# A new order of stages for every engine of a two-layer transformer kernel, and GpSimd's squares and products in halves

## The chip, the core and the metric

One core of a Trainium2 chip runs the whole program in one launch. The metric is device microseconds (us), the median of three runs. Engines are named TensorE (PE; its weight loads PEld), VectorE (DVE), ScalarE (ACT), GpSimd (POOL) and SyncE (SP, which only issues DMAs here). Each takes its instructions strictly in the order in which the program lists them, and waits on semaphores for the others.

## The reference

The input is 32 entries of 256 tokens by 128 channels, float32. Per entry, with layer norm in front of each layer:

```python
xn = _layernorm(x, axis=-1)
x = x + _L0_attn_ref(xn, ...) + _L0_ffn_ref(xn, ...)
xn = _layernorm(x, axis=-1)
x = x + _L1_attn_ref(xn, ...) + _L1_ffn_ref(xn, ...)
```

`_L0_attn_ref` is 16-head attention over normalised q and k whose weight is `(1 - arccos(clip(q.k)) / pi) ** 16`, divided by the row sum. `_L0_ffn_ref` is a second 16-head attention, with softmax, plus a mixture of 8 experts of which the gate picks 2. `_L1_attn_ref` is causal single-head attention. `_L1_ffn_ref` is a gated MLP (128 to 352 to 128) whose operands are rounded to FP4 in blocks of 16 along the last axis. No entry needs another.

## The kernel before

Weights are prepared once (transposes, FP4 rounding), up to about 50 us. Then the program runs steps t = -1 to 33. The work on an entry is cut into stages, and the table `ORDER` holds for each engine a list of `(stage, argument, lag)`: in step t the engine does that stage for entry t + lag. A stage with lag +1 is so done a step ahead of one with lag 0, and lag -2 is the last. `steps` unrolls steps -1, 0, 1 and the last ones and loops over two steps at a time between them; items whose entry doesn't exist are skipped. The lists are the only thing that sets the order; nothing is moved at run time.

The stages that matter here, in the order in which an entry goes through them:

- `load` (SP), `ln0` (VectorE moments, ScalarE a first guess of 1/sd), `rstd0` (VectorE refines it, L774 to L776), `xnT` (VectorE writes the normalised tile `xn`, L781; TensorE transposes it; ScalarE copies it to `xnT`), `proj` 0 and 1 (TensorE; ScalarE copies one bank, VectorE the other, L802).
- `gmax`, `gexp`, `choose` 0 to 4: the gate. `choose` 1 is a copy of 4 numbers a row, L836.
- `norm`, `guess`, `newton`, `unit`, `high`, `stack`, `stackT`: q and k are normalised, cut into a float16 high and low part (ScalarE or GpSimd copy the high part, GpSimd subtracts, L566) and transposed.
- `m` 0 to 7: scores whose row maximum VectorE takes (L885); `maxT`: these maxima are cut into bfloat16 parts by VectorE (L897 to L900), transposed by TensorE and copied by ScalarE; `e` 0 to 7: the scores again less the maximum, ScalarE's exponential (`prob`); `pvf`: their product with v.
- `c` 0 to 7: cosines, which VectorE clips into `curve` (L879). For each of four pairs: `sq` (GpSimd squares, L530), `ln` and `sigm` (ScalarE), `mul` (curve times root: pairs 0 and 2 on GpSimd, L533; 1 and 3 on VectorE, L875), `arctan`, `wln`, `wexp` (ScalarE), `pvw`. `table` 0 and 1 load ScalarE's function table before the logarithms and the sigmoids.
- `experts` 0 and 1 (TensorE; VectorE adds 16 tiles, L859), `finf`, `finc`, `ocT`, `wo`: outputs of layer 0.
- `ln1` (as `ln0`; ScalarE writes `rstd1`), `rstd1`, `xn1T`, `quantx` 0 to 8 (FP4 rounding in nine small steps; step 7 is L452), `xqT`, `p1`, `gu`, `hmul`, `quanth` 0 to 8, `hT`, `s1`, `s1e`, `p1T`, `o1`, `down`, and the store from SP.

Scores go through two PSUM slots in turn (`SCORES`), and all else of TensorE through two banks in turn (`MISC`), both counted in the order of TensorE's list: a stage on TensorE waits (`bank_read`) until what used its slot or bank last has been read. A new list for TensorE therefore changes these waits too.

GpSimd's two stages that the change touches are the `sq` and `mul` branches of its `run`.

## Time and profile before

| | before |
|---|---|
| median of 3 runs | 1975.3 us (1971.95 to 1977.01) |
| the profiled execution | 1968.91 us, its span 1967.1 us |
| busy over the span | ACT 1778.4, DVE 1761.1, PE 1475.6, POOL 1183.2 us |
| mean granted TensorE clock | 0.856 |
| time from step to step, t = 1 to 32 | 57.61 us (1786.0 us over 31 steps) |

The span is nearly all repetition: a step of every engine, 31 times over, with a ramp of some 70 us in front (weights, steps -1 and 0) and the drain of the last entry behind. So the time is read from one step. A time stamp in the rows is in us from the span's start; "idle before" is time in which the engine stood, with what ended it behind the arrow. Two rows of one engine can overlap by about 0.1 us, since an instruction starts while the one ahead of it is ending.

### The profile page before, as it was taken

What the parts mean: (1) busy time and instruction counts of PE and PEld (TensorE: products, weight loads), DVE (VectorE), ACT (ScalarE), POOL (GpSimd) and SP (SyncE); (2) the same over time, 40 slices, a digit from 0 to 9 for tenths busy, and PEclk for the clock granted to TensorE, in tenths of its full rate; (3) what the DMA queues carried; (4) which work ended last, traced back from release to release, by engine and by line L of the source; (5) the groups of instructions that cost most, each with busy time, mean ns of one, the idle gap of its engine ahead of it and who ended that gap; (6) DMA issues with size and microseconds to landing.
All of it is one profiled execution on the core that took longest, in us unless ns stands there. A gap on an engine that the chain in (4) does not pass through costs nothing.

```text
span 1967.1 us, 38505 instructions
## 1 busy us (share of the span) xinstructions
PE 1475.6 (75%) x12022; PEld 751.1 (38%) x12022; DVE 1761.1 (90%) x3977; ACT 1778.4 (90%) x1888; POOL 1183.2 (60%) x540
## 2 busy tenths in 40 slices
PE   2677778777778777777878777778778778777765
PEld 1223434333443433344343334434334434333333
DVE  5779998999999999999999999999999999999864
ACT  1299999999999999999999999999999999999993
POOL 1556666666666666666666656665666666665640
PEclk9667898889888988988898888898888888888876
DMA  1000000000000000000000000000000000000000
GB/s 42 3 4 1 6 1 6 5 6 6 6 5 0 6 5 6 6 6 5 0 6 5 6 6 6 0 6 6 5 6 5 6 0 6 6 5 6 4 3 6
DMA packets 21058, 11.19 MB, mean 6 GB/s; under 512 B 1431, under 2 KB 20953, under 8 KB 20956
## 3 DMA queue, kind: packets, MB, share of 16 engines
q1 hardware_dynamic: 20956, 10.20, 1.8%
q14 instruction: 83, 0.68, 0.1%
...
## 4 chain that ended last, share of the span: by engine, by line
DVE 37%; issue 22%; ACT 20%; PE 18%; DVEq 2%; SPq 0%; POOL 0%; ACTq 0%; DMA 0%; POOLq 0%
ACT curve L578 10%; DVE nmax L885 6%; DVE curve L875 5%; ACT root L578 4%; PE psM L1045 4%; DVE curve L879 3%; PE psM L1037 3%; DVE acc L859 3%; DVE xn L781 1%; PE psS L1095 1%; DVE h L454 1%; PE psM L1207 1%; PE psM L1190 1%; DVE stkT L871 1%; ACT prob L578 1%
## 5 line engine op out<-in xcount | busy, mean ns | idle before, releaser
L530 POOL TENSOR_TENSOR root<-curve 128x2048 f32<-128x2048 f32 x128 | 478.9, 3741 | 453.2 <-DVE curve L879 453.2
L578 ACT ACTIVATE curve<-curve 128x2048 f32<-128x2048 f32 x384 | 719.1, 1907 | 5.6 <-POOL curve L533 2.2
L578 ACT ACTIVATE root<-root 128x2048 f32<-128x2048 f32 x256 | 484.7, 1906 | 0.0
L533 POOL TENSOR_TENSOR curve<-curve,root 128x2048 f32<-128x2048 f32 x64 | 354.6, 5562 | 65.2 <-ACT root L578 65.2
L879 DVE TENSOR_SCALAR curve<-psS 128x1024 f32<-128x1024 f32 x256 | 308.2, 1215 | 2.7 <-PE psS L1068 1.9
L885 DVE TENSOR_REDUCE nmax<-psS 128x4 f32<-128x1024 f32 x256 | 302.7, 1213 | 0.9 <-PE psS L1077 0.9
L578 ACT ACTIVATE prob<-psS 128x1024 f32<-128x1024 f32 x256 | 256.6, 1029 | 32.8 <-PE psS L1097 31.1
L566 POOL TENSOR_TENSOR stk<-qk,stk 128x512 f16<-128x512 f32 x128 | 148.1, 1167 | 73.4 <-ACT stk L578 72.9
L1045 PE MATMUL psM<-we,xnT 128*128 128x512 f32 x256 | 172.4, 762 | 0.0
L875 DVE TENSOR_TENSOR curve<-curve,root 128x2048 f32<-128x2048 f32 x64 | 161.0, 2516 | 6.1 <-ACT root L578 6.1
L1077 PE MATMUL psS<-stkT 32*128 32x256 f16 x1024 | 103.1, 294 | 80.7 <-DVE curve L879 42.5
L1221 PE MATMUL psV<-curve,vc 128*32 128x256 f32 x2048 | 134.1, 391 | 26.1 <-ACT curve L578 22.4
L1190 PE MATMUL psM<-wguT,xqT 128*128 128x352 f32 x256 | 124.6, 624 | 36.3 <-ACT hqT L578 32.9
L1221 PE MATMUL psV<-prob,vf 128*32 128x256 f32 x2048 | 151.0, 417 | 0.6 <-ACT prob L578 0.6
L859 DVE SCALAR_TENSOR_TENSOR acc<-psM,comb,acc 128x128 f32<-128x128 f32 x512 | 136.8, 337 | 12.2 <-PE psM L1045 11.8
L1207 PE MATMUL psM<-wdT,hqT 128*128 128x128 f32 (+1 forms) x384 | 88.6, 416 | 64.1 <-DVE h L977 63.4
L1068 PE MATMUL psS<-stkT 32*128 32x256 f16 x1024 | 105.6, 316 | 22.6 <-DVE curve L879 11.7
L1207 PEld LDWEIGHTS psM<-wdT,hqT 128*128 128x128 f32 (+1 forms) x384 | 79.4, 312 | 77.9 <-DVE h L977 76.8
L1056 PE MATMUL psM<-ident,stk 128*128 128x128 f16 x1024 | 81.8, 225 | 33.6 <-ACT xn1T L578 25.8
L1095 PE MATMUL psS<-stkT 32*128 32x256 f16 x1024 | 102.8, 300 | 3.4 <-ACT prob L578 2.3
L1097 PE MATMUL psS<-mT,pickb 32*128 32x256 bf16 x1024 | 102.2, 299 | 0.0
L1221 PEld LDWEIGHTS psV<-curve,vc 128*32 128x32 f32 x2048 | 59.9, 110 | 98.0 <-issue 71.7
...
## 6 DMA issues: line engine op xcount, KB each, us to landing
...
```

The costliest lines, as they stand in the source:

```text
L530: nc.gpsimd.tensor_tensor(root[:, two], curve[:, p, two], curve[:, p, two], ALU.mult).then_inc(s_sq, 1)
L533: nc.gpsimd.tensor_tensor(curve[:, p, two], curve[:, p, two], root[:, two], ALU.mult).then_inc(s_half[0], 1)
L566: nc.gpsimd.tensor_tensor(lo, src, hi, ALU.subtract).then_inc(s_stk, 1)
L578: return nc.scalar.activation(out, in_, func, **kw)
L859: nc.vector.scalar_tensor_tensor(acc[:, p, j, :], bank[:, (e % 4) * D:(e % 4 + 1) * D], comb[:, p, j, e:e + 1], acc[:, p, j, :], ALU.mult, ...
L875: nc.vector.tensor_tensor(curve[:, p, two], curve[:, p, two], root[:, two], ALU.mult).then_inc(s_half[1], 1)
L879: nc.vector.tensor_scalar(curve[:, p, arg * UC:(arg + 1) * UC], psS[:, slot_of(stage, arg), :, :, :].rearrange("p a k q -> p (a k q)"), CO ...
L885: nc.vector.tensor_reduce(nmax[:, :, 2 * arg:2 * arg + 2].rearrange("p j a -> p a j"), psS[:, slot_of(stage, arg), :, :, :], AX.X, ALU.max ...
L1045: mm(bank[:, :], xnT[:, j * P:(j + 1) * P], we[:, 4 * arg:4 * arg + 4, :].rearrange("p e f -> p (e f)"), start=False, stop=True).then_inc( ...
L1190: ins = mm(bank[:, 0:I], xqT[:, arg * P:(arg + 1) * P], wguT[:, m, :], start=True, stop=True)
L1207: ins = mm(bank[:, j * D:(j + 1) * D], hqT[0:CH[c], j, c, :], wdT[0:CH[c], c, :], start=(c == 0), stop=(c == NCH - 1))
L1221: ins = mm(psV[rows(hh), kind, half, :], head_window(v, p, kt, head_at(g, hh)), w[:, hh, kt, :], start=(g % 2 == 0 and kt == 0), stop=(g % ...
```

## The change

Every engine but SP gets a new list. Each list is turned (a step now begins with `wln` 1 on ScalarE, `experts` 0 on VectorE, `c` 4 on TensorE, and `sq` 1 on GpSimd), so a few stages have another lag, and the stages inside are permuted. GpSimd's `sq` and `mul` over 2048 elements a row become two instructions over 1024 each; the semaphore is raised by the second.

```diff
@@ -56,44 +56,43 @@
         ("load", 0, 1), ("down", 0, -2),
     ],
     "tensor": [
-        ("c", 2, 0), ("s1", 0, -2), ("finf", 0, -1), ("c", 3, 0), ("c", 4, 0), ("experts", 0, 0), ("c", 5, 0),
-        ("pvw", 0, -1), ("c", 6, 0), ("experts", 1, 0), ("pvw", 1, -1), ("pvw", 2, -1), ("p1T", 0, -2),
-        ("pvw", 3, -1), ("xnT", 0, 1), ("maxT", 0, 0), ("c", 7, 0), ("proj", 0, 1), ("e", 0, 0), ("proj", 1, 1),
-        ("e", 1, 0), ("finc", 0, -1), ("o1", 0, -2), ("ocT", 0, -1), ("e", 2, 0), ("e", 3, 0), ("wo", 0, -1),
-        ("pvf", 0, 0), ("e", 4, 0), ("e", 5, 0), ("pvf", 1, 0), ("xn1T", 0, -1), ("e", 6, 0), ("e", 7, 0),
-        ("stackT", 0, 1), ("stackT", 1, 1), ("pvf", 2, 0), ("m", 0, 1), ("m", 1, 1), ("p1", 0, -1), ("m", 2, 1),
-        ("stackT", 2, 1), ("pvf", 3, 0), ("stackT", 3, 1), ("m", 3, 1), ("xqT", 0, -1), ("m", 4, 1), ("hT", 0, -2),
-        ("hT", 1, -2), ("c", 0, 1), ("gu", 0, -1), ("m", 5, 1), ("m", 6, 1), ("gu", 1, -1), ("c", 1, 1), ("m", 7, 1),
-        ("down", 0, -2),
+        ("c", 4, 0), ("s1", 0, -2), ("experts", 0, 0), ("pvw", 0, -1), ("c", 5, 0), ("c", 6, 0), ("maxT", 0, 0),
+        ("experts", 1, 0), ("e", 0, 0), ("e", 1, 0), ("pvw", 1, -1), ("pvw", 2, -1), ("p1T", 0, -2), ("c", 7, 0),
+        ("xnT", 0, 1), ("pvw", 3, -1), ("proj", 0, 1), ("proj", 1, 1), ("e", 2, 0), ("o1", 0, -2), ("e", 3, 0),
+        ("finc", 0, -1), ("pvf", 0, 0), ("hT", 0, -2), ("e", 4, 0), ("ocT", 0, -1), ("e", 5, 0), ("wo", 0, -1),
+        ("hT", 1, -2), ("pvf", 1, 0), ("e", 6, 0), ("stackT", 0, 1), ("e", 7, 0), ("stackT", 1, 1), ("m", 0, 1),
+        ("xn1T", 0, -1), ("m", 1, 1), ("m", 2, 1), ("stackT", 2, 1), ("pvf", 2, 0), ("m", 3, 1), ("stackT", 3, 1),
+        ("m", 4, 1), ("pvf", 3, 0), ("m", 5, 1), ("xqT", 0, -1), ("p1", 0, -1), ("c", 0, 1), ("gu", 0, -1),
+        ("c", 1, 1), ("m", 6, 1), ("gu", 1, -1), ("c", 2, 1), ("m", 7, 1), ("finf", 0, 0), ("down", 0, -2),
+        ("c", 3, 1),
     ],
     "vector": [
-        ("c", 2, 0), ("s1", 0, -2), ("finf", 0, -1), ("quanth", 1, -2), ("c", 3, 0), ("c", 4, 0), ("quanth", 2, -2),
-        ("experts", 0, 0), ("c", 5, 0), ("quanth", 3, -2), ("ln0", 0, 1), ("c", 6, 0), ("experts", 1, 0),
-        ("quanth", 4, -2), ("rstd0", 0, 1), ("quanth", 5, -2), ("xnT", 0, 1), ("maxT", 0, 0), ("quanth", 6, -2),
-        ("quanth", 7, -2), ("c", 7, 0), ("proj", 0, 1), ("proj", 1, 1), ("gmax", 0, 1), ("quanth", 8, -2),
-        ("finc", 0, -1), ("o1", 0, -2), ("norm", 0, 1), ("wo", 0, -1), ("ln1", 0, -1), ("rstd1", 0, -1),
-        ("choose", 0, 1), ("xn1T", 0, -1), ("quantx", 0, -1), ("newton", 0, 1), ("quantx", 1, -1), ("quantx", 2, -1),
-        ("choose", 1, 1), ("quantx", 3, -1), ("quantx", 4, -1), ("stackT", 0, 1), ("quantx", 5, -1),
-        ("quantx", 6, -1), ("stackT", 1, 1), ("choose", 2, 1), ("quantx", 7, -1), ("m", 0, 1), ("m", 1, 1),
-        ("quantx", 8, -1), ("p1", 0, -1), ("choose", 3, 1), ("m", 2, 1), ("stackT", 2, 1), ("stackT", 3, 1),
-        ("m", 3, 1), ("m", 4, 1), ("mul", 1, 0), ("c", 0, 1), ("hmul", 0, -1), ("m", 5, 1), ("m", 6, 1),
-        ("mul", 3, 0), ("hmul", 1, -1), ("choose", 4, 1), ("quanth", 0, -1), ("c", 1, 1),
-        ("m", 7, 1), ("down", 0, -2),
+        ("experts", 0, 0), ("c", 5, 0), ("c", 6, 0), ("ln0", 0, 1), ("experts", 1, 0), ("rstd0", 0, 1),
+        ("quanth", 5, -2), ("xnT", 0, 1), ("quanth", 6, -2), ("c", 7, 0), ("quanth", 7, -2), ("proj", 0, 1),
+        ("quanth", 8, -2), ("proj", 1, 1), ("gmax", 0, 1), ("o1", 0, -2), ("finc", 0, -1), ("choose", 0, 1),
+        ("norm", 0, 1), ("wo", 0, -1), ("ln1", 0, -1), ("rstd1", 0, -1), ("xn1T", 0, -1), ("newton", 0, 1),
+        ("stackT", 0, 1), ("quantx", 0, -1), ("stackT", 1, 1), ("quantx", 1, -1), ("choose", 1, 1), ("quantx", 2, -1),
+        ("quantx", 3, -1), ("m", 0, 1), ("quantx", 4, -1), ("choose", 2, 1), ("quantx", 5, -1), ("quantx", 6, -1),
+        ("quantx", 7, -1), ("m", 1, 1), ("choose", 3, 1), ("quantx", 8, -1), ("choose", 4, 1), ("m", 2, 1),
+        ("stackT", 2, 1), ("m", 3, 1), ("stackT", 3, 1), ("m", 4, 1), ("m", 5, 1), ("p1", 0, -1), ("mul", 1, 0),
+        ("c", 0, 1), ("hmul", 0, -1), ("c", 1, 1), ("m", 6, 1), ("mul", 3, 0), ("m", 7, 1), ("hmul", 1, -1),
+        ("c", 2, 1), ("quanth", 0, -1), ("finf", 0, 0), ("quanth", 1, -1), ("maxT", 0, 1), ("quanth", 2, -1),
+        ("down", 0, -2), ("quanth", 3, -1), ("c", 3, 1), ("quanth", 4, -1), ("s1", 0, -1), ("c", 4, 1),
     ],
     "scalar": [
-        ("table", 0, -1), ("wln", 0, -1), ("wln", 1, -1), ("wexp", 0, -1), ("s1e", 0, -2), ("wexp", 1, -1),
-        ("wln", 2, -1), ("wexp", 2, -1), ("wln", 3, -1), ("ln0", 0, 1), ("wexp", 3, -1), ("p1T", 0, -2), ("ln", 0, 0),
-        ("xnT", 0, 1), ("maxT", 0, 0), ("ln", 1, 0), ("proj", 0, 1), ("oC", 0, -1), ("e", 0, 0), ("proj", 1, 1),
-        ("e", 1, 0), ("ln", 2, 0), ("ocT", 0, -1), ("gexp", 0, 1), ("e", 2, 0), ("e", 3, 0), ("guess", 0, 1),
-        ("ln1", 0, -1), ("e", 4, 0), ("e", 5, 0), ("ln", 3, 0), ("xn1T", 0, -1), ("e", 6, 0), ("high", 2, 1),
-        ("e", 7, 0), ("high", 3, 1), ("table", 1, 0), ("p1", 0, -1), ("sigm", 0, 0), ("sigm", 1, 0), ("xqT", 0, -1),
-        ("sigm", 2, 0), ("hT", 0, -2), ("hT", 1, -2), ("arctan", 0, 0), ("gu", 0, -1), ("sigm", 3, 0), ("oF", 0, 0),
-        ("arctan", 1, 0), ("gu", 1, -1), ("arctan", 2, 0), ("arctan", 3, 0),
+        ("wln", 1, -1), ("wexp", 0, -1), ("wln", 2, -1), ("wexp", 1, -1), ("wexp", 2, -1), ("maxT", 0, 0),
+        ("wln", 3, -1), ("s1e", 0, -2), ("ln0", 0, 1), ("e", 0, 0), ("wexp", 3, -1), ("p1T", 0, -2), ("xnT", 0, 1),
+        ("e", 1, 0), ("oC", 0, -1), ("proj", 0, 1), ("ln", 0, 0), ("proj", 1, 1), ("e", 2, 0), ("ln", 1, 0),
+        ("gexp", 0, 1), ("e", 3, 0), ("hT", 0, -2), ("ocT", 0, -1), ("e", 4, 0), ("e", 5, 0), ("guess", 0, 1),
+        ("hT", 1, -2), ("ln1", 0, -1), ("e", 6, 0), ("e", 7, 0), ("ln", 2, 0), ("high", 2, 1), ("ln", 3, 0),
+        ("high", 3, 1), ("xn1T", 0, -1), ("table", 1, 0), ("sigm", 0, 0), ("sigm", 1, 0), ("xqT", 0, -1),
+        ("p1", 0, -1), ("sigm", 2, 0), ("sigm", 3, 0), ("gu", 0, -1), ("oF", 0, 0), ("arctan", 0, 0),
+        ("arctan", 1, 0), ("arctan", 2, 0), ("gu", 1, -1), ("arctan", 3, 0), ("table", 0, 0), ("wln", 0, 0),
     ],
     "gpsimd": [
-        ("fadd", 0, -1), ("sq", 2, 0), ("sq", 3, 0), ("norm", 0, 1), ("high", 0, 1), ("high", 1, 1), ("stack", 0, 1),
-        ("stack", 1, 1), ("unit", 0, 1), ("stack", 2, 1), ("stack", 3, 1), ("residual", 0, 1), ("mul", 0, 0),
-        ("mul", 2, 0), ("sq", 0, 1), ("sq", 1, 1),
+        ("sq", 1, 0), ("fadd", 0, -1), ("sq", 2, 0), ("sq", 3, 0), ("norm", 0, 1), ("high", 0, 1), ("high", 1, 1),
+        ("stack", 0, 1), ("stack", 1, 1), ("unit", 0, 1), ("stack", 2, 1), ("stack", 3, 1), ("mul", 0, 0),
+        ("mul", 2, 0), ("residual", 0, 1), ("sq", 0, 1),
     ],
 }
 MOST_LAG = max(-lag for order in ORDER.values() for s, a, lag in order)
@@ -523,14 +522,16 @@
             pool.wait_ge(s_wcp, SETUP_USES)
 
             def run(stage, arg, b, p, t):
-                two = slice(arg * 2 * UC, (arg + 1) * 2 * UC)
+                one, other = (slice((2 * arg + k) * UC, (2 * arg + k + 1) * UC) for k in range(2))
                 if stage == "sq":
                     pool.wait_ge(s_clip, due(s_clip, b, 2 * arg + 2))
                     pool.wait_ge(*half_done(b - 1, arg))
-                    nc.gpsimd.tensor_tensor(root[:, two], curve[:, p, two], curve[:, p, two], ALU.mult).then_inc(s_sq, 1)
+                    nc.gpsimd.tensor_tensor(root[:, one], curve[:, p, one], curve[:, p, one], ALU.mult)
+                    nc.gpsimd.tensor_tensor(root[:, other], curve[:, p, other], curve[:, p, other], ALU.mult).then_inc(s_sq, 1)
                 if stage == "mul" and arg not in HALF_ON_DVE:
                     pool.wait_ge(s_sig, due(s_sig, b, arg + 1))
-                    nc.gpsimd.tensor_tensor(curve[:, p, two], curve[:, p, two], root[:, two], ALU.mult).then_inc(s_half[0], 1)
+                    nc.gpsimd.tensor_tensor(curve[:, p, one], curve[:, p, one], root[:, one], ALU.mult)
+                    nc.gpsimd.tensor_tensor(curve[:, p, other], curve[:, p, other], root[:, other], ALU.mult).then_inc(s_half[0], 1)
                 if stage == "residual":
 
                     pool.wait_ge(s_x[p], due(s_x[p], b, LANDED[p]))
```

## Rows read from the trace of the kernel before

**Rows 1.** The page: busy us of each engine (share of the span) xinstructions.

```profile
PE 1475.6 (75%) x12022; PEld 751.1 (38%) x12022; DVE 1761.1 (90%) x3977; ACT 1778.4 (90%) x1888; POOL 1183.2 (60%) x540
```

**Rows 2.** One line's instructions (min/median/max ns): the table load that opens a step.

```profile
L609 ACT ACT_TABLE_LOAD  x32: 1283/1283/1283, 124.4 to 1910.4; - x32
```

**Rows 3.** Stretches (us, busy and count by engine, clock): 23 steps; half clock.

```profile
411.90:1739.70 1327.80, 1035.65 (x8627) 529.25 (x8627) 1241.20 (x2807) 1268.43 (x1335) 846.97 (x368) 0.87 0.02 5
...
1228.00:1231.40 3.40, 3.40 (x5) 0.77 (x4) 3.36 (x8) 3.37 (x3) 2.96 (x2) 0.50 0.01 2
```

**Rows 4.** Waits in 411.9 to 1739.7: us in total, times, longest.

```profile
ACT prob L578 <- PE psS L1097: 22.3, 43, 1.3
ACT ocT L578 <- PE psM L1122: 16.7, 23, 1.0
```

**Rows 5.** Timeline of ScalarE in one step (start, length, [idle before]).

```profile
1236.48 0.38 ACT L578 ACTIVATE xnT<-psM 128x256 f32<-128x256 f32 x1
1237.33 0.38 ACT L578 ACTIVATE mT<-psM 128x256 bf16<-128x256 bf16 x1 [0.47 <-PE psM L1087]
...
1249.39 0.20 ACT L578 ACTIVATE lnv<-mv 128x2 f32<-128x2 f32 x1 [0.16 <-DVE mv L768]
1249.62 0.20 ACT L578 ACTIVATE rstd<-lnv 128x2 f32<-128x2 f32 x1
1249.81 1.94 ACT L578 ACTIVATE prob<-psS 128x1024 f32<-128x1024 f32 x2
1251.63 1.91 ACT L578 ACTIVATE root<-root 128x2048 f32<-128x2048 f32 x1
...
1254.60 0.65 ACT L578 ACTIVATE stk<-qk 128x512 f16<-128x512 f32 x1
...
1294.53 0.37 ACT L578 ACTIVATE xnT<-psM 128x256 f32<-128x256 f32 x1
```

**Rows 6.** Timeline of VectorE in the same step.

```profile
1235.70 0.23 DVE L897 CAST mstk<-nmax 128x32 bf16<-128x32 f32 x1
...
1236.49 0.30 DVE L900 TENSOR_TENSOR mstk<-nres,mstk 128x32 bf16<-128x32 f32 x1
...
1249.86 0.16 DVE L774 SCALAR_TENSOR_TENSOR lnt<-mv,rstd 128x2 f32<-128x2 f32 x1 [0.51 <-ACT rstd L578]
...
1250.33 0.16 DVE L831 TENSOR_REDUCE gs<-ge 128x2 f32<-128x16 f32 x1
...
1256.29 0.47 DVE L452 SCALAR_TENSOR_TENSOR xq<-xqT,xq 128x256 f32<-128x256 f32 x1
...
1290.02 1.90 DVE L859 SCALAR_TENSOR_TENSOR acc<-psM,comb,acc 128x128 f32<-128x128 f32 x7 [0.36 <-PE psM L1045]
...
1293.16 0.59 DVE L781 TENSOR_SCALAR xn<-xt,mv,rstd 128x128 f32<-128x128 f32 x2
```

**Rows 7.** One line's instructions each: VectorE beside GpSimd (min/median/max ns).

```profile
L836 DVE COPY best<-top x32: 160/892/896, 55.9 to 1833.8; 128x4 f32<-128x4 f32 x32
L452 DVE SCALAR_TENSOR_TENSOR xq<-xqT,xq x32: 424/592/1296, 161.5 to 1940.5; 128x256 f32<-128x256 f32 x32
L875 DVE TENSOR_TENSOR curve<-curve,root x64: 2279/2466/4924, 113.2 to 1904.2; 128x2048 f32<-128x2048 f32 x64
```

**Rows 8.** One line's instructions each: GpSimd's prices (min/median/max ns).

```profile
L530 POOL TENSOR_TENSOR root<-curve x128: 3601/3602/4181, 70.2 to 1877.7; 128x2048 f32<-128x2048 f32 x128
L533 POOL TENSOR_TENSOR curve<-curve,root x64: 4519/5556/6616, 109.2 to 1899.4; 128x2048 f32<-128x2048 f32 x64
L543 POOL TENSOR_TENSOR qsq<-qk x32: 1041/1773/1776, 50.2 to 1823.3; 128x512 f32<-128x512 f32 x32
```

**Rows 9.** Timeline of TensorE: one expert matmul pair at each clock.

```profile
1222.04 1.13 PE L1045 MATMUL psM<-we,xnT 128*128 128x512 f32 x2
...
1227.79 1.95 PE L1045 MATMUL psM<-we,xnT 128*128 128x512 f32 x2
```

**Rows 10.** Timeline of ScalarE in the ramp, step 0.

```profile
81.75 0.20 ACT L578 ACTIVATE lnv<-mv 128x2 f32<-128x2 f32 x1 [23.34 <-DVE mv L768]
```

## The prediction

> **What bounds the kernel now.** First the page: ScalarE and VectorE are each busy for 90% of the span, TensorE for 75%, GpSimd for 60% [rows 1]. So no transfer matters, and the question is what lies in the idle tenth of the two. Next the period: the table load that opens ScalarE's step comes 32 times, from 124.4 to 1910.4 us [rows 2], so a step takes 1786.0 / 31 = 57.61 us. In the 23 steps from 411.9 to 1739.7, ScalarE is busy 1268.43 / 23 = 55.15 us a step and VectorE 1241.20 / 23 = 53.97 us [rows 3]. A new order can't take less than ScalarE's 55.15 us, so at most 2.5 us a step are to be had. ScalarE's largest waits are for TensorE's scores, 22.3 / 23 = 0.97 us a step, and for the transposed output, 0.73 us [rows 4].
>
> Then the timelines, for the loop that sets the period; the reader is to see that two engines hand it to each other. ScalarE writes the second layer norm's rstd at 1249.82 [rows 5]; VectorE, which stood 0.51 us for it, goes on at 1249.86 and works through most of its list until the next entry's `xn` is written at 1293.75 [rows 6]. That is stretch A, 43.93 us. TensorE transposes it and ScalarE takes it at 1294.53, 0.78 us later [rows 5]. From `xnT` at 1236.48 to rstd at 1249.82 ScalarE then has stretch C, 13.34 us, in which VectorE has slack. 43.93 + 0.78 + 13.34 = 58.05, within 0.8% of the mean step. A microsecond that VectorE waits in A, or ScalarE in C, is a microsecond of the period; the other way round it is hidden.
>
> **The change, part by part.**
>
> **Stretch A.** Comparing the two lists of VectorE from `rstd1` to `xnT`: the new one has all stages of the old, plus `maxT`, less `choose` 0. `maxT` costs 1.09 us from first to last, about 1.0 with the overlap [rows 6]; `choose` 0 is three short overlapping instructions, the first 0.16 us long [rows 6], some 0.2 in all. In the old list `choose` 1, a copy of 4 numbers, takes 0.89 us where 0.16 would do [rows 7], since GpSimd works on the same memory beside it; in the new list it falls into a gap of GpSimd (after `unit`, before the third `stack`): -0.73. The two multiplications of VectorE took 2.47 where 2.28 is their least [rows 7], 2 x 0.19 = 0.37; I find them at the end of a GpSimd product in the new order too, but with halves the rest to wait for is shorter: 0.2 stays, so -0.2. The wait for experts of 0.36 [rows 6] goes, if TensorE is at 2.4 GHz there. Sum: 43.93 + 1.0 - 0.2 - 0.73 - 0.2 - 0.36 = 43.4 us. I take 43.5, with 0.1 for `xn1T` standing right behind `rstd1`. Bounds: 43.2 if no wait is left, 44.7 if as much time is lost to GpSimd as now (0.73 + 0.37) and 0.2 more.
>
> **Stretch C.** Of the 13.34 us five waits, of which the first, 0.47, and the last, 0.16, stand in the rows, make 2.37 [rows 5]; 10.97 are work. The new list has in C five exponentials for four (+0.91, half of the 1.82 us from start of two to the next instruction), `hT` twice (+0.76), and not `maxT` (-0.28): 12.36; with two waits less, 0.2 more is saved by overlap. Three waits remain in the new list: for `proj` 0, which TensorE now has behind `pvw` 3; for `e` 2, behind `proj` 1; and for `ocT`, behind `e` 4. Before, `e` and `ocT` alone made 0.97 + 0.73 [rows 4]; I put all three at half of that, 0.85, an estimate. 12.16 + 0.85 = 13.0 us. Bounds: 12.5 with 0.3 of waits, 14.5 with the 2.37 of now.
>
> **What ScalarE itself needs in A.** What C gains in work ScalarE's part of A loses (1.4 us), so its path has 1.4 us of cover there. That hides a new wait: TensorE now has `xqT` behind `m` 5, which waits for VectorE to read `m` 3; `p1`, `c` 0 and `gu` are queued behind it, and ScalarE stands up to 0.7 us for `xqT`. If VectorE is over 1 us late there, the cover is used up.
>
> The table load with `wln` 0, and `finf`, only change the step in which they are counted. SP's list is as it was: its loads wait for sums two entries back, its stores for `down`, and neither is near the loop.
>
> **GpSimd in halves.** Of a square of 512 elements (1.041 us at the least) and one of 2048 (3.602) [rows 8] I work out 1.67 ns an element and 0.19 us that each instruction costs by itself. Six more instructions a step cost 1.1 us, between 0 (if they overlap) and 2. GpSimd is busy 846.97 / 23 = 36.8 us of 57.6 [rows 3], so this is hidden unless `arctan` 2 waits for it. The first product starts with ScalarE's `sigm` 0, some 10.0 us after rstd; two products of 4.52 + 0.15 [rows 8] with one of VectorE's between them (2.28) end at 21.6. ScalarE's own list reaches `arctan` 2 at 20.4 without waits and 21.1 with `xqT`'s: 0.5 to 1.2 us, inside its cover of 1.4. If that cover is gone, it is paid.
>
> **Ramp and drain.** In step 0 ScalarE stands 23.34 us before `ln0` [rows 10]. With `maxT` a step earlier it can do two exponentials in that time, 1.8 us, and VectorE's `xn` comes earlier: 3 us, between 0 and 6. The drain is one entry's chain in both: 0.
>
> **The clock.** Between 1228.0 and 1231.4 the granted clock is 0.50, so 1.2 GHz [rows 3], and a pair of expert matmuls takes 1.95 us against 1.13 [rows 9]. The new list puts TensorE's work from `finf` through `stackT` 1 close together, and I take 2.4 GHz for it.
> The Trainium skill ("TensorE: Matmul & The Clock Gate", Part 1: The HAM clock gate) says that for modelling the ramp penalty is under 1% of a typical kernel's span and shouldn't be fitted. By that rule an order laid with the clock in it brings under 20 us, and the result stays near the time before. The trace agrees for the time and not for the share: the mean clock is 0.87, yet ScalarE's two waits above come to 1.7 us a step.
>
> **The sum.** 43.5 + 0.78 + 13.0 = 57.3 us a step, 0.3 less than 57.61; over 31 steps -10, with the ramp -13. The profiled execution took 1968.9 us (span 1967.1 and 1.8 around it), so 1956 us; the median of the runs is 6.4 us above that execution, so the median should be 1962 us. With the gain between -1.1 and +0.9 us a step, 1935 to 2002.
>
> **The rivals.**
>
> *GpSimd's last subtraction gets in front of `quantx` 7 (slower).* In the old step L452 comes 6.43 us after L774 [rows 6]. In the new list `m` 0 stands ahead of it (+1.13), `choose` 0 doesn't (-0.22), nor `choose` 1's wait (-0.73), with 0.1 for the gap: 6.7 us after rstd. GpSimd's last `stack` starts when ScalarE's last `high` is done: two exponentials (1.82), two logarithms of 1.91 less the overlap of 0.1, and two copies of 0.65, the first less its overlap [rows 5]: 6.6 us, and the start. If GpSimd is first, VectorE waits for all of that instruction, as in the executions of L452 that took up to 1296 ns instead of 424 [rows 7]. 0.85 us a step: +0.55 net, 31 x 0.55 - 3 = +14, so 1989 us. It decides at less than 0.1 us, and half of L452's executions took under 592 ns: 25%.
> The Trainium skill ("SBUF — State Buffer", SBUF: two separate sides) calls the pair of ports that VectorE and GpSimd share an exclusive lock: whoever starts first has it for the whole instruction. By that rule the loser pays all of the rest, in each step alike, which is this rival; the trace agrees, with 0.89 us for the copy of 4 numbers.
>
> *TensorE falls to 1.2 GHz in the dense part (slower).* Both halves of `experts` 1 wait for reads by VectorE and ScalarE; at 1.95 for 1.13 us a pair [rows 9] the second bank is two times 0.82, 1.6 us, late, and VectorE waits in A. +1.3 us a step net, 31 x 1.3 - 3 = +37: 2012 us. It decides when TensorE has stood for VectorE's `hmul` 1 and the clock has not come back by `experts` 1. 9%.
>
> *ScalarE takes over (no change).* The waits for `xqT`, the products and TensorE use up its 1.4 us of cover: 57.6 us a step, 1972 to 1975 us. For it: ScalarE reached 1294.53 without any wait, so it was as late as VectorE. 16%.
>
> *The order holds better than I find (faster).* No wait of VectorE on GpSimd, a third of those in C: 43.2 + 0.78 + 12.5 = 56.5, -34 - 3: 1938 us. 10%.
>
> **How the numbers follow.** My forecast, 1962 us, has 40% (its own range 1948 to 1974). A measurement can't tell 0.3%, 6 us, from no change. Faster by more: most of the forecast's 40% and the last rival, 48%. Within: the third rival and the edges of its neighbours, 20%. Slower: the first two and the far part of the third, 32%. The range 1935 to 2002 leaves out the worst of the clock and more than 56.5.
>
> **What would show it.** ScalarE's table loads 57.3 us apart; L836 at 0.16 us; L452 near 424 ns (near 1296 ns: the first rival); ScalarE's waits for scores and `ocT` together under 1.0 us a step; L1045 near 1.13 us a pair throughout (1.95: the second rival). GpSimd busy about 1.1 us a step longer. I am wrong at the root if stretch A isn't what ends the step, which waits of VectorE inside A would show.

## The result, and the profile after

The changed kernel takes 1992.8 us (median of 4 runs, 1991.9 to 1996.2) against 1973.7 us of the kernel before on the same chip: a ratio of 1.0095, with a 95% interval of 1.0077 to 1.0112. It is slower by 1%, where 1962 us was predicted. The profiled execution took 1993.0 us, with a span of 1991.2.

The page's busy line answers to [rows 1]:

```profile
PE 1513.1 (76%) x12022; PEld 748.9 (38%) x12022; DVE 1763.2 (89%) x3977; ACT 1774.6 (89%) x1888; POOL 1253.6 (63%) x732
```

VectorE and ScalarE do what they did before, in 24 us more of span. The table load that opens ScalarE's step (now L610) answers to [rows 2]:

```profile
L610 ACT ACT_TABLE_LOAD  x32: 1283/1283/1283, 129.2 to 1933.7; - x32
```

So a step takes (1933.7 - 129.2) / 31 = 58.21 us where it took 57.61: 18.5 of the 24 us. The first load comes 4.8 us later, and after the last one 57.5 us follow for 56.7. The loss is in the loop, and some of it in the ramp.

One line's instructions each (min/median/max ns), against [rows 7] and [rows 8]; line numbers in the helper for fp4 have gone down by one, most of the others up by one:

```profile
L837 DVE COPY best<-top x32: 159/165/167, 57.2 to 1855.5; 128x4 f32<-128x4 f32 x32
...
L451 DVE SCALAR_TENSOR_TENSOR xq<-xqT,xq x32: 424/1341/1416, 167.7 to 1963.2; 128x256 f32<-128x256 f32 x32
...
L876 DVE TENSOR_TENSOR curve<-curve,root x64: 2280/2346/3603, 117.0 to 1923.9; 128x2048 f32<-128x2048 f32 x64
...
L529 POOL TENSOR_TENSOR root<-curve x128: 1884/1894/3937, 69.1 to 1897.3; 128x1024 f32<-128x1024 f32 x128
```

The copy of 4 numbers is at its least (0.89 us before), but `quantx` 7 (L451) now takes 1.34 us in the median, where 0.42 would do. ScalarE's waits from 420 to 1770 us (in total, times, longest), to be read beside [rows 4]:

```profile
ACT xqT L579 <- PE psM L1183: 48.6, 23, 2.7
ACT prob L579 <- PE psS L1098: 5.5, 16, 0.5
ACT u1T L579 <- PE psM L1146: 4.1, 14, 0.5
ACT ocT L579 <- PE psM L1123: 4.0, 23, 0.2
```

The waits for scores and for `ocT` are nearly gone (1.70 us a step before, 0.41 now), and one for `xqT` of 2.1 us a step has come, where the old kernel's was under 0.1. What happens on VectorE and GpSimd around `quantx` 7 (timeline of one step; ScalarE's rstd ended at 1326.75):

```profile
1332.94 0.42 DVE L449 SCALAR_TENSOR_TENSOR xq<-xqT,xq 128x256 f32<-128x256 f32 x1
1333.40 1.40 DVE L451 SCALAR_TENSOR_TENSOR xq<-xqT,xq 128x256 f32<-128x256 f32 x1
1334.73 1.21 DVE L886 TENSOR_REDUCE nmax<-psS 128x4 f32<-128x1024 f32 x1
```

```profile
1333.36 1.16 POOL L567 TENSOR_TENSOR stk<-qk,stk 128x512 f16<-128x512 f32 x1 [1.16 <-ACT stk L579]
```

GpSimd's last `stack` starts 0.04 us ahead of `quantx` 7, which then ends 0.28 us after it. In all 23 steps from 411.9 to 1739.7 us it starts ahead, by 0.04 to 0.10 us. ScalarE a little later in the same step:

```profile
1336.69 1.90 ACT L579 ACTIVATE root<-root 128x2048 f32<-128x2048 f32 x1
1340.16 0.38 ACT L579 ACTIVATE xqT<-psM 128x256 f32<-128x256 f32 x1 [1.58 <-PE psM L1183]
1340.69 0.38 ACT L579 ACTIVATE u1T<-psM 128x256 f32<-128x256 f32 x1 [0.15 <-PE psM L1146]
```

TensorE has `xqT` behind `m` 5, which waits until VectorE has read `m` 3. VectorE comes to `m` 3 later by what `quantx` 7 lost.

The prediction measured one step of the old kernel in three pieces. The same three over the 23 middle steps of either kernel, from the starts of ScalarE's `xnT`, the ends of its second rstd and the ends of VectorE's `xn`:

| us a step | step measured then | before, mean of 23 | forecast | after, mean of 23 |
|---|---|---|---|---|
| stretch A (rstd to `xn`) | 43.93 | 44.15 | 43.5 | 44.70 |
| TensorE's transposes and `xnT` | 0.78 | 1.00 | 0.78 | 0.87 |
| stretch C (`xnT` to rstd) | 13.34 | 12.58 | 13.0 | 12.58 |
| sum | 58.05 | 57.73 | 57.3 | 58.15 |

The three pieces lie end to end, so they add up to the step by definition; what counts is which of them changed. A has grown, C is what it was. The steps aren't alike: 11 of the 23 take 57.4 to 57.6 us, the others up to 59.7.

### The profile page after: what moved, and what is told of

The parts are those of the page before. It is cut to its first block and busy times, and to the rows that moved or that the text cites. A ratio compares the mean times of both kernels' runs of the same rounds, so it can differ in the third digit from the quotient of the medians.

```text
span 1991.2 us, 38613 instructions
## 1 busy us (share of the span) xinstructions
PE 1513.1 (76%) x12022; PEld 748.9 (38%) x12022; DVE 1763.2 (89%) x3977; ACT 1774.6 (89%) x1888; POOL 1253.6 (63%) x732
## 5 line engine op out<-in xcount | busy, mean ns | idle before, releaser
L579 ACT ACTIVATE curve<-curve 128x2048 f32<-128x2048 f32 x384 | 710.2, 1903 | 7.9 <-POOL curve L534 7.0
L529 POOL TENSOR_TENSOR root<-curve 128x1024 f32<-128x1024 f32 x128 | 266.3, 2081 | 305.5 <-DVE curve L880 305.5
L533 POOL TENSOR_TENSOR curve<-curve,root 128x1024 f32<-128x1024 f32 x64 | 193.4, 3022 | 147.9 <-ACT root L579 147.9
L579 ACT ACTIVATE prob<-psS 128x1024 f32<-128x1024 f32 x256 | 255.9, 1024 | 15.8 <-PE psS L1098 13.6
L1078 PE MATMUL psS<-stkT 32*128 32x256 f16 x1024 | 131.0, 347 | 181.0 <-DVE stkT L872 71.3
L530 POOL TENSOR_TENSOR root<-curve 128x1024 f32<-128x1024 f32 x128 | 261.4, 2042 | 0.0
L1222 PE MATMUL psV<-prob,vf 128*32 128x256 f32 x2048 | 178.2, 478 | 0.0
L1046 PE MATMUL psM<-we,xnT 128*128 128x512 f32 x256 | 156.0, 694 | 0.0
L534 POOL TENSOR_TENSOR curve<-curve,root 128x1024 f32<-128x1024 f32 x64 | 152.6, 2385 | 0.0
L1078 PEld LDWEIGHTS psS<-stkT 32*128 32x128 f16 x1024 | 32.3, 100 | 279.4 <-DVE nmax L886 124.7
L1096 PE MATMUL psS<-stkT 32*128 32x256 f16 x1024 | 115.0, 281 | 4.4 <-ACT prob L579 4.2
L1114 PE MATMUL psM<-ident,oFs 128*128 128x128 f32 x128 | 34.1, 422 | 110.1 <-DVE h L978 110.1
L1098 PE MATMUL psS<-mT,pickb 32*128 32x256 bf16 x1024 | 113.1, 278 | 0.0
L1057 PE MATMUL psM<-ident,stk 128*128 128x128 f16 x1024 | 101.2, 257 | 5.4 <-POOL stk L567 5.3
```

What stands on the lines that cost most here:

```text
L529: nc.gpsimd.tensor_tensor(root[:, one], curve[:, p, one], curve[:, p, one], ALU.mult)
L530: nc.gpsimd.tensor_tensor(root[:, other], curve[:, p, other], curve[:, p, other], ALU.mult).then_inc(s_sq, 1)
L533: nc.gpsimd.tensor_tensor(curve[:, p, one], curve[:, p, one], root[:, one], ALU.mult)
L534: nc.gpsimd.tensor_tensor(curve[:, p, other], curve[:, p, other], root[:, other], ALU.mult).then_inc(s_half[0], 1)
L579: return nc.scalar.activation(out, in_, func, **kw)
L1046: mm(bank[:, :], xnT[:, j * P:(j + 1) * P], we[:, 4 * arg:4 * arg + 4, :].rearrange("p e f -> p (e f)"), start=False, stop=True).then_inc( ...
```

## The experiments

Each ratio is against the kernel before, run on the same chip beside it. The changed kernel stands at 1.0095.

### The lock on `quantx` 7

```diff
-        ("quantx", 7, -1), ("m", 1, 1), ("choose", 3, 1), ("quantx", 8, -1), ("choose", 4, 1), ("m", 2, 1),
+        ("m", 1, 1), ("quantx", 7, -1), ("choose", 3, 1), ("quantx", 8, -1), ("choose", 4, 1), ("m", 2, 1),
```

> The new order, with VectorE's m 1 (a read of PSUM) one place ahead of quantx 7 (L451), so that quantx 7 comes after GpSimd's last stack. Theory (the lock on quantx 7 is the loss, and it also makes TensorE's xqT late for ScalarE): L451 falls from a mean of 1.28 us to under 0.5, ScalarE's wait for xqT from 2.1 to about 1.2 us a step, and a step takes about 0.85 us less, so 31 x 0.85 = 26 us: 1966 us, ratio to the kernel before 0.996. Rival (ScalarE's own work and another wait set the step, and VectorE only fills what is left): L451 falls just the same, but the time stays within 6 us of 1993, ratio 1.007 to 1.012.

Measured: 1975.3 us, ratio 0.9999 (0.9985 to 1.0014). `quantx` 7 and the table load:

```profile
L451 DVE SCALAR_TENSOR_TENSOR xq<-xqT,xq x32: 407/415/424, 167.8 to 1940.3; 128x256 f32<-128x256 f32 x32
...
L610 ACT ACT_TABLE_LOAD  x32: 1283/1283/1283, 128.3 to 1911.5; - x32
```

One exchange of two neighbours gives back the whole loss: the last GpSimd subtraction now runs beside a read of PSUM, which it doesn't hold up (VectorE, then GpSimd):

```profile
1203.00 1.22 DVE L886 TENSOR_REDUCE nmax<-psS 128x4 f32<-128x1024 f32 x1
```

```profile
1203.08 1.15 POOL L567 TENSOR_TENSOR stk<-qk,stk 128x512 f16<-128x512 f32 x1 [1.16 <-ACT stk L579]
```

The gain is 0.96%, 19 us, between the theory's 26 and the rival's 6, nearer to the theory. The exchange also frees the slot of `m` 1 earlier, so the ratio alone doesn't single out the lock. Steps of the short kind do: stretch A takes 44.1 to 44.3 us in them with the lock and 43.15 to 43.3 without, 1.0 us less, and nearly all of that is the length of `quantx` 7 itself (1.34 to 1.40 us for 0.41). The wait for `xqT` only fell to 1.5 us a step, and the steps come in two kinds: 11 of the 23 take 56.5 to 56.6 us, 12 take 58.0 to 58.3. What makes the others long is taken up below.

### Work for ScalarE while `xqT` is late

```diff
-        ("high", 3, 1), ("xn1T", 0, -1), ("table", 1, 0), ("sigm", 0, 0), ("sigm", 1, 0), ("xqT", 0, -1),
-        ("p1", 0, -1), ("sigm", 2, 0), ("sigm", 3, 0), ("gu", 0, -1), ("oF", 0, 0), ("arctan", 0, 0),
+        ("high", 3, 1), ("xn1T", 0, -1), ("table", 1, 0), ("sigm", 0, 0), ("sigm", 1, 0), ("sigm", 2, 0),
+        ("xqT", 0, -1), ("p1", 0, -1), ("sigm", 3, 0), ("gu", 0, -1), ("oF", 0, 0), ("arctan", 0, 0),
```

> The new order, with ScalarE's sigm 2 (1.9 us) ahead of xqT, so that ScalarE has work while TensorE's xqT is late; quantx 7 stays locked. Theory (VectorE's stretch A sets the step, ScalarE only just keeps up): the wait for xqT goes from 2.1 us a step to under 0.5, but only what ScalarE is late at xnT comes back, 0.87 less 0.63 us, some 0.25 us a step with the 1.2 GHz steps a little more: 6 to 16 us, 1977 to 1987 us, ratio 1.002 to 1.007. Rival (ScalarE's wait for xqT is itself the loss): 1.5 us a step or more, under 1950 us, ratio under 0.99.

Measured: 2036.9 us, ratio 1.0312 (1.0287 to 1.0338). Neither the theory nor the rival had it: 44 us were lost, not 6 to 16 won. The wait for `xqT` did go, to 0.45 us a step, but another took its place:

```profile
ACT curve L579 <- DVE curve L876: 55.6, 23, 2.7
...
ACT xqT L579 <- PE psM L1183: 10.4, 13, 0.9
```

The timelines of GpSimd and of VectorE's multiplication in one step show why:

```profile
1245.03 2.37 POOL L533 TENSOR_TENSOR curve<-curve,root 128x1024 f32<-128x1024 f32 x1 [2.34 <-ACT root L579]
1247.35 2.37 POOL L534 TENSOR_TENSOR curve<-curve,root 128x1024 f32<-128x1024 f32 x1
1249.66 2.37 POOL L533 TENSOR_TENSOR curve<-curve,root 128x1024 f32<-128x1024 f32 x1
1251.97 4.43 POOL L534 TENSOR_TENSOR curve<-curve,root 128x1024 f32<-128x1024 f32 x1
```

```profile
1250.58 3.59 DVE L876 TENSOR_TENSOR curve<-curve,root 128x2048 f32<-128x2048 f32 x1
```

With `sigm` 2 done early, GpSimd's second product follows the first without a gap. VectorE's multiplication arrives in its first half and takes 3.59 us for 2.28; the second half then takes 4.43 for 2.35. The multiplication ends 2.1 us after the first half, and the second half 2.2 us after the multiplication: each waited for the other in turn. In the changed kernel the wait for `xqT` had held GpSimd back: there the second product starts 0.5 to 1.4 us behind VectorE's multiplication in all 23 steps.

> Both edits: m 1 ahead of quantx 7, and sigm 2 ahead of xqT. Theory (VectorE is the limit until the lock is gone, then both are within 0.3 us): a step of 57.0 to 57.2 us, that is 26 + 8 us off 1993, 1959 us with 1952 to 1966 as bounds, ratio 0.990 to 0.996. Rival (one limit alone): no better than the better one of the two edits by itself, within 4 us.

This was both edits. Measured: 2039.8 us, ratio 1.0325 (1.0298 to 1.0353), no better than the second alone, and far from what the theory and the rival said: the multiplications are slow in this kernel too (a median of 4.2 us for the first). The test of the explanation holds the second product until VectorE's first multiplication is done:

```diff
                     pool.wait_ge(s_sig, due(s_sig, b, arg + 1))
+                    if arg == 2:
+                        pool.wait_ge(*half_done(b, 1))
```

> Both first edits (m 1 ahead of quantx 7, sigm 2 ahead of xqT), and GpSimd's second product waits until VectorE's first multiplication is done. Theory (the 43 us that sigm 2 ahead of xqT cost came only from GpSimd's second product, which then started straight behind the first and took the memory from VectorE's multiplication, 3.1 to 3.6 us instead of 2.28): both multiplications are back at 2.3 to 2.5 us, a step takes 56.5 to 57.6 us, 1944 to 1980 us, ratio 0.984 to 1.003. Rival (moving sigm 2 costs by ScalarE's own order, u1T and gu being later): over 2015 us, ratio over 1.02.

Measured: 1988.4 us, ratio 1.0061 (1.0037 to 1.0085). Of the 3.25 points the hold brings back 2.6; the first multiplication is at 2.28 us again (the second at 2.60 to 2.67). So the collision on GpSimd was the loss of the second experiment. The time is still 8 us above the theory's range: every one of the 23 steps now takes 58.0 us, the long kind, and in each the granted clock stands at 0.50 from about 17.5 to 27.7 us after `xnT`. What is left goes with the clock; that ScalarE's order has no part in it was not tested.

### The two halves of the change, alone

> The new order, but GpSimd's squares and products whole again, as before. Theory (the halves are hidden and beside the point; the loss is the order's): 1993 us within 6, ratio 1.006 to 1.013, GpSimd busy about 1.1 us a step less, VectorE's two multiplications (L876) up to 0.2 us a step longer. Rival (the halves cost the time, by more starts of GpSimd that get in front of VectorE): over 6 us faster, ratio under 1.006. Other rival (the halves are what lets VectorE's multiplications in): over 10 us slower, ratio over 1.014.

The new order with whole GpSimd instructions: 2000.2 us, ratio 1.0132 (1.0107 to 1.0157). The halves don't cost; with the new order they seem worth some 7 us, by intervals that just overlap. What they gain is in stretch C (13.25 us whole, 12.58 in halves), and some of it is lost again in A (44.45 whole, 44.70 in halves). ScalarE's waits in the kernel with whole instructions, from 420 to 1770 us, are:

```profile
ACT ocT L577 <- PE psM L1121: 9.7, 23, 0.4
ACT hqT L577 <- PE psM L1197: 6.9, 21, 0.4
```

With halves `ocT` has 4.0 and `hqT` doesn't appear.

> The old order, with GpSimd's squares and products as two instructions each (the other part of the change alone). Theory (the halves alone matter little: they add 1.1 us a step to GpSimd, hidden, and let VectorE's two multiplications in up to 0.2 us sooner): 0 to 0.4 us a step less, 1963 to 1976 us, ratio 0.994 to 1.001. Rival (each additional start of a GpSimd instruction is one more chance to get in front of VectorE): 0.3 us a step or more, ratio over 1.005.

The old order with halves: 1978.1 us, ratio 1.0015 (1.0001 to 1.0028), near no change. So the loss is the order's.

### What makes the long steps

TensorE in a long step of the kernel with `m` 1 first (`xnT` at 1410.10, the next at 1468.21):

```profile
1423.38 0.62 PE L1057 MATMUL psM<-ident,stk 128*128 128x128 f16 x8
1426.21 0.39 PE L1078 MATMUL psS<-stkT 32*128 32x256 f16 x4 [2.22 <-DVE stkT L872]
1426.54 0.44 PE L1139 MATMUL psM<-ident,xn 128*128 128x128 f32 x2
1426.90 0.39 PE L1078 MATMUL psS<-stkT 32*128 32x256 f16 x4
1428.09 0.60 PE L1078 MATMUL psS<-stkT 32*128 32x256 f16 x4 [0.79 <-DVE nmax L886]
1428.63 1.03 PE L1057 MATMUL psM<-ident,stk 128*128 128x128 f16 x8
1429.59 1.94 PE L1222 MATMUL psV<-prob,vf 128*32 128x256 f32 x16
...
1435.90 0.69 PE L1183 MATMUL psM<-ident,xq 128*128 128x128 f32 x2
```

After idle stretches of 2.22 and 0.79 us the same `m` takes 0.60 for 0.39, `stackT` 1.03 for 0.62, `pvf` 1.94 for 1.07: that is 1.2 for 2.4 GHz. From `m` 2 on TensorE is busy throughout and late with `xqT`, which comes 25.8 to 26.0 us after `xnT` in long steps and 24.4 to 24.9 in short ones. The two idle stretches alone don't make a step long: four short steps of this kernel have them as well. The stretch from 20 to 28 us after `xnT` in a short step (`xnT` at 1353.49) and in this long one; the columns are the stretch, its length, busy time and count of PE, PEld, DVE, ACT and POOL, the granted clock, and DMA:

```profile
1373.50:1381.50 8.00, 7.87 (x68) 3.58 (x60) 8.00 (x13) 7.27 (x7) 5.26 (x4) 0.84 0.00 0
1430.10:1438.10 8.00, 8.00 (x64) 3.75 (x56) 7.01 (x12) 5.34 (x6) 4.95 (x3) 0.53 0.00 1
```

In all 23 steps of that kernel: 0.78 or more in this stretch goes with 56.45 to 56.62 us, 0.57 or less with 58.0 to 58.3. The changed kernel itself has the same split: 0.79 or more with 57.4 to 57.6 us (11 steps), 0.62 or less with 57.9 to 59.7 (12 steps). In the kernel before, the same stretch, in which its `xqT` lies too, had 0.94 or more in all 23 steps: the new order brought the fall into this chain. All this is a correlation. Four kernels moved work to test it, and three then added to TensorE's activity without moving any.

```diff
-        ("m", 4, 1), ("pvf", 3, 0), ("m", 5, 1), ("xqT", 0, -1), ("p1", 0, -1), ("c", 0, 1), ("gu", 0, -1),
+        ("m", 4, 1), ("m", 5, 1), ("xqT", 0, -1), ("p1", 0, -1), ("pvf", 3, 0), ("c", 0, 1), ("gu", 0, -1),
```

> The new order with m 1 ahead of quantx 7 (as in the first experiment), and TensorE's pvf 3 (1.07 us at 2.4 GHz, 1.93 at 1.2) moved from between m 4 and m 5 to behind p1, so that it is not ahead of xqT and p1. In the first experiment the steps came in two kinds, 56.5 us and 58.1 us, the long ones with a clock of 0.65 from m 2 to xqT against 1.00. Theory (in the long steps TensorE at 1.2 GHz is late with xqT for ScalarE and with p1 for VectorE): the long steps lose 1.2 us or more, mean step 56.5 to 56.9, 1944 to 1958 us, ratio 0.984 to 0.991. Rival (the long steps come from elsewhere, and the clock only goes with them): the two kinds stay, 1968 to 1978 us, ratio 0.997 to 1.002. Other rival (ScalarE's earlier sigm 2 lets GpSimd's second product in front of VectorE's multiplication, as in the second experiment): over 1985 us, ratio over 1.005.

Measured, with `m` 1 first: 1974.0 us, ratio 0.9995 (0.9979 to 1.0010). The wait for `xqT` halved (17.7 us in 23 steps), but the mean step stayed at 57.6 us (57.4 before the move). That is the first rival's time, but the two kinds didn't stay as they were. The clock still fell in the chain, and in 12 of the 23 steps once more 51 to 52 us after `xnT`; those 12 take 57.8 to 58.0 us, and the waits for scores and experts grew. Of the steps without that second fall, one in which the first lasts from 17.2 to 27.4 us takes 57.1 us, and two in which it lasts to 30.6 take 59.2. A lighter chain alone doesn't cure the long steps.

```diff
-        ... ("e", 7, 0), ("stackT", 1, 1), ("m", 0, 1),
-        ("xn1T", 0, -1), ("m", 1, 1), ("m", 2, 1), ("stackT", 2, 1), ("pvf", 2, 0), ("m", 3, 1), ("stackT", 3, 1),
-        ("m", 4, 1), ("pvf", 3, 0), ("m", 5, 1), ("xqT", 0, -1), ...
+        ... ("e", 7, 0), ("stackT", 1, 1), ("pvf", 2, 0), ("pvf", 3, 0), ("m", 0, 1),
+        ("xn1T", 0, -1), ("m", 1, 1), ("m", 2, 1), ("stackT", 2, 1), ("m", 3, 1), ("stackT", 3, 1),
+        ("m", 4, 1), ("m", 5, 1), ("xqT", 0, -1), ...
```

> The new order with m 1 ahead of quantx 7, and TensorE's pvf 2 and pvf 3 moved out of the m chain into the gap of 2.2 us in which TensorE stands between stackT 1 and m 0. In the three kernels seen with m 1 ahead, a step is 56.5 us long where the granted clock falls to 0.50 some 17 us after xnT for 3.4 to 6.9 us, and 58.0 to 58.3 us where it stays there for 10.2 us. Theory (1.2 GHz in the m chain, with the two pvf in it, is what makes the long steps; with the gap filled and the chain light it no longer matters): every step 56.4 to 56.8 us, 1942 to 1955 us, ratio 0.983 to 0.990. Rival (the clock falls anyway, and what is late moves on to gu or to experts): steps of 57.4 us and more, ratio over 0.994.

> The new order with the two pvf moved into the gap ahead of m 0 alone, quantx 7 where the change put it. Theory (the lock and the clock are two separate losses): the lock on L451 stays at 1.3 us, the long steps of 58.4 to 59.6 go, every step is 57.4 to 57.6 us, 1968 to 1978 us, ratio 0.997 to 1.002. Rival (the long steps of the changed kernel come from the lock, by the later m chain, not from the clock): 1985 us or more, ratio over 1.005.

> All edits: m 1 ahead of quantx 7, sigm 2 ahead of xqT with GpSimd's second product held until VectorE's first multiplication is done, and the two pvf in the gap ahead of m 0. With the hold alone, every step had 10.2 us at a granted clock of 0.50 and took 58.0 us. Theory (VectorE's list sets the step once lock and clock are out of the way, ScalarE has over 1 us of cover): 56.3 to 56.7 us a step, within 4 us of the kernel with the two pvf moved but without sigm 2 and hold, ratio 0.983 to 0.990. Rival (ScalarE and VectorE are both at their limit there, and ScalarE's earlier sigm 2 brings more): 55.8 us a step or less, ratio under 0.978. Other rival (GpSimd's second product ends too late for arctan 2): over 57.2 us a step, ratio over 0.994.

With `m` 1 first: 1981.7 us, ratio 1.0041 (1.0025 to 1.0058). With the lock kept: 1990.9 us, 1.0088 (1.0061 to 1.0116). With `sigm` 2 and the hold: 1991.3 us, 1.0094 (1.0066 to 1.0122). By their times all three go to a rival: the fall moves from 17 to between 19 and 21 us after `xnT` and then mostly lasts until 29 to 31, over `xqT`, `p1` and `gu`. The reasons that the rivals gave aren't all borne out. In the second, with the lock kept, the granted clock is at 0.50 from 20 to 28 us after `xnT` in every step, so its steps of 58.0 us don't show the lock without the clock. In the third GpSimd's product, which its rival blamed, is not among ScalarE's larger waits; the largest is for `gu`, 54.4 us. In the first VectorE waits for experts, 17.5 us from 420 to 1770 us where the kernel of the first experiment has 0.3:

```profile
DVE acc L860 <- PE psM L1046: 17.5, 20, 1.1
```

In these kernels, moving work only moved the fall. The next kernel adds activity and moves nothing: TensorE repeats `stackT` 1 and `m` 1, the same result in the same place, before anyone reads it.

```diff
-                    for g in range(4):
+                    for g in 3 * list(range(4)) if arg == 1 else range(4):
...
-                    for qt_ in range(NT):
+                    for qt_ in list(range(NT)) * {1: 3}.get(arg, 1):
```

> The new order with m 1 ahead of quantx 7, every list as in the first experiment, and TensorE does some work again, with the same result in the same place: the transposes of stackT 1 three times (1.2 us more, in the gap of 2.2 us ahead of m 0) and m 1 three times (0.8 us more, in the gap ahead of m 2). VectorE reads neither before the repeats are done. So nothing changes but TensorE's activity. Theory (TensorE's idle time ahead of the m chain is what the fall of the clock follows, and the clock is what makes the long steps): the fall comes later than 17 us after xnT or is shorter, and the share of long steps (58.0 us and more, 12 to 14 of 23) falls; if all go, 56.5 us a step, 1946 us, ratio 0.986; over half gone, under 0.994. Rival (the fall only moves, as with the two pvf, and gu or experts are late instead): 57.5 us a step or more, ratio 0.998 to 1.006.

Measured, with `m` 1 first: 1958.0 us (1957.1 to 1958.9), ratio 0.9909 (0.9887 to 0.9930). TensorE in one step, and the table load:

```profile
1363.26 0.39 PE L1078 MATMUL psS<-stkT 32*128 32x256 f16 x4 [1.33 <-DVE stkT L872]
1363.59 0.44 PE L1139 MATMUL psM<-ident,xn 128*128 128x128 f32 x2
1363.95 0.83 PE L1078 MATMUL psS<-stkT 32*128 32x256 f16 x12
1365.13 0.39 PE L1078 MATMUL psS<-stkT 32*128 32x256 f16 x4 [0.35 <-DVE nmax L886]
```

```profile
L610 ACT ACT_TABLE_LOAD  x32: 1283/1283/1283, 130.5 to 1898.2; - x32
```

The idle stretches are down to 1.33 and 0.35 us. In 20 of the 23 steps the fall is later or lasts about 3 us; 4 steps are long where 12 were, and the mean step is 57.02 us by the table loads. Nothing but TensorE's own activity differs from the first experiment, and the two kinds keep their lengths (most short steps 56.5 to 56.6 us, and 58.1 to 58.3 in the three that still have the long fall in the chain). So the clock is a cause of the long steps, and having fewer of them is worth 0.9% of the time. This version is faster than both kernels.

> As the kernel with stackT 1 and m 1 three times, and m 2, m 3 and m 4 twice as well (0.39 us each at 2.4 GHz, 0.60 at 1.2). Theory (with TensorE busy throughout the m chain the clock stays, and at 2.4 GHz the repeats end before VectorE reads): 56.4 to 56.7 us a step, ratio 0.984 to 0.990. Rival (the clock falls anyway; then the chain has 1.8 us more of work at 1.2 GHz, which all comes ahead of xqT and p1): long steps of 59.5 us and more, ratio over 1.01.

`m` 2, `m` 3 and `m` 4 twice as well: 1965.6 us, ratio 0.9957 (0.9939 to 0.9975), between the two. Neither expectation holds for the whole, and each for a part: 17 of the 23 steps take 56.5 to 56.6 us, as the theory had it, and 6, in which the clock falls all the same, take 59.0 to 59.1, near the rival's 59.5.

> The changed kernel with TensorE's stackT 1 and m 1 three times each, as before, and with quantx 7 where the change put it (so L451 stays at 1.3 us). Theory (lock and clock are two losses that add): of the steps of 58.3 to 59.7 us at most a quarter stays, mean step 57.5 to 57.8, 31 x 0.5 = 16 us off 1993, 1972 to 1982 us, ratio 0.998 to 1.004. Rival (the clock is a loss only when the lock is gone, since the lock keeps VectorE the later one anyway): 1988 us or more, ratio over 1.007.

Measured: 2013.7 us, ratio 1.0190 (1.0166 to 1.0214), 20 us worse than the changed kernel. That lies within the rival's bound, but its reason, that the clock doesn't matter while the lock stays, would give no change and not a loss. TensorE in one step, and the granted clock over the start of the chain and over the rest of it:

```profile
1226.30 0.83 PE L1078 MATMUL psS<-stkT 32*128 32x256 f16 x12
1227.48 0.39 PE L1078 MATMUL psS<-stkT 32*128 32x256 f16 x4 [0.35 <-DVE nmax L886]
...
1231.24 0.39 PE L1078 MATMUL psS<-stkT 32*128 32x256 f16 x4 [1.82 <-DVE nmax L886]
1231.56 0.62 PE L1057 MATMUL psM<-ident,stk 128*128 128x128 f16 x8
1232.88 0.60 PE L1078 MATMUL psS<-stkT 32*128 32x256 f16 x4 [0.69 <-DVE nmax L886]
1233.41 1.93 PE L1222 MATMUL psV<-prob,vf 128*32 128x256 f32 x16
```

```profile
1222.00:1231.00 9.00, 5.74 (x84) 3.57 (x80) 8.70 (x26) 8.97 (x9) 3.39 (x3) 1.00 0.00 0
1232.50:1240.50 8.00, 7.62 (x40) 3.77 (x40) 7.16 (x8) 4.81 (x5) 5.11 (x3) 0.57 0.00 1
```

In 18 of the 23 steps, as here, the repeats did hold the clock up to `m` 3. There TensorE stands 1.82 us for VectorE's read of `m` 1, which is late by the lock on `quantx` 7 (still 1.40 us), and the clock falls over the rest of the chain instead. No step takes less than 58.35 us, and ScalarE's wait for `xqT` has grown from 2.1 to 2.7 us a step. So lock and clock are not two losses that add: with the lock kept, the repeats cost 20 us instead of bringing some. This account is read from the trace; no run tested it.

## Why the prediction was wrong

The time lies inside the stated range, but it went the other way than forecast.

**The period.** Right: the step is set by a loop of A, the transposes and C. At the end of C VectorE stood for ScalarE's rstd in all 23 steps (19.5 us), and a microsecond taken out of A in the first experiment shortened like steps by a microsecond. ScalarE reached `xnT` without a wait in 19 of the 23 steps, so both engines are at the limit, as the third rival had it; but what makes ScalarE late is the wait for `xqT`, which VectorE and TensorE set.

**Stretch A, the step that failed.** Its sum left out the lock on `quantx` 7, that is, it put that wait of VectorE on GpSimd at nothing. The first rival had the mechanism and its price, 0.85 us a step (0.93 by the median row); what was wrong was the chance it was given. That the rival's 1989 us is so near the 1992.8 measured is partly luck: it has C 0.42 us a step too long, the ramp 7.8 us too short, and no price for the clock in the `m` chain. The working put `quantx` 7 at 6.7 us after rstd and the last `stack` at 6.6 us "and the start"; they come at 6.65 and 6.61. So its own sum had GpSimd ahead, by about 0.1 us where 0.04 was measured, and the 25% treated that as a toss. Both paths run from the same rstd over instructions of nearly fixed length, and the order was the same in all 23 steps. That half of the old executions were short said nothing, since the old order had another distance. The Trainium skill ("SBUF — State Buffer", SBUF: two separate sides) has the shared pair of ports as an exclusive lock for the whole instruction; the trace agrees, as 1.34 us against 0.415 with the two exchanged shows. It ends 0.28 us behind the subtraction and not 0.415, so a part of it wasn't held up.

The other terms of A held, and so did the signs named for them: `best` at 0.165 us (-0.73), the multiplications at a median of 2.35 us (forecast 2.38), and little waiting for experts (2.5 us in the 23 steps). With the lock gone, in the short steps of the first experiment, A is 43.15 to 43.3 us, at the lower bound of 43.2.

**The clock in A.** The second rival, 1.2 GHz, was given 9% and one place, `experts` 1. There the clock stayed up in 19 of the 23 steps; in the other 4, of 59.5 to 59.7 us, it fell there too, and the matmuls' lateness cost VectorE at most 0.8 us, where 1.6 was the rival's price. Mostly it fell in the `m` chain, a place that the argument took no price for. An estimate from the short steps (57.5 us) and the mean (58.15) is 0.65 us a step, 20 us, 1.0% of the span. The sentence of the Trainium skill that the prediction drew on ("TensorE: Matmul & The Clock Gate", Part 1: The HAM clock gate) is on the slow matmuls at a kernel's start. It sets no bound on a fall that comes back in every step, and nothing in the trace of the kernel before could bear out a time for an order laid with the clock in it.

**`xqT` behind `m` 5.** Named, and mis-sized: at most 0.7 us forecast, 2.1 measured, above the cover of 1.4. The prediction said that over 1 us of lateness of VectorE would use the cover up; the lock's 0.93 us and TensorE at the low clock together did.

**Stretch C.** 13.0 us forecast, 12.58 measured, and yet no gain: the mean of the old steps was 12.58 too. I measured one step of 58.05 us and held its pieces against the mean step of 57.61, which looked within 0.8%; but its C was 0.76 us longer than the mean, and its A and transposes 0.44 shorter. The saving of 0.34 us that the forecast counted in C lay in the choice of that step.

**GpSimd's halves.** The price of an instruction was right: two squares of 1.894 us for one of 3.602, 0.19 more. GpSimd's busy time grew by 70.4 / 32 = 2.2 us a step, not 1.1, but not by the halves: squares and products together take 1.2 us a step more, near the forecast. The rest is mostly `residual`, a sum that now stands behind the products and takes 2.6 us on the mean for 0.73. By the timelines it nearly always starts 0.2 us behind VectorE's second multiplication; in the second experiment, where it comes 2.1 us ahead of that, it takes 0.72. The longer busy time is hidden, as forecast (0.06 us a step of waits of ScalarE for L534).

**Ramp.** -3 us forecast, +4.8 measured. ScalarE in step 0, against [rows 10]:

```profile
81.14 0.38 ACT L579 ACTIVATE mT<-psM 128x256 bf16<-128x256 bf16 x1 [23.01 <-PE psM L1088]
83.94 0.20 ACT L579 ACTIVATE lnv<-mv 128x2 f32<-128x2 f32 x1 [2.42 <-DVE mv L769]
...
87.19 1.02 ACT L579 ACTIVATE prob<-psS 128x1024 f32<-128x1024 f32 x1 [2.81 <-PE psS L1098]
90.48 0.38 ACT L579 ACTIVATE xnT<-psM 128x256 f32<-128x256 f32 x1 [2.27 <-PE psM L1030]
```

`maxT` stands ahead of `ln0` now, on VectorE too, so that `lnv` is 2.2 us later and `xnT` 2.9 (87.56 before); I had counted ScalarE's time saved and not what VectorE does first. The rest to 4.8 us is, by the trace, VectorE's two multiplications of step 0 (3.60 and 3.36 us) and the product behind them, for which ScalarE waits 1.98 us. This was read from the trace alone; no run tried it.

**The sum.** A +1.20, transposes +0.09, C -0.42: 0.87 us a step, 27 us. The ramp adds 7.8 and the drain 0.8; 1.5 us lie in the steps outside the middle 23. Together 37, from the 1956 us forecast for the profiled execution to its 1993.

What stays open: which idle stretches the clock's fall follows and how long it lasts was not settled; the runs only show that it moves with TensorE's work. Nor is it settled why the repeats with the lock kept cost 20 us.
